# Attention quads in pairs on one Trainium2 core: scores alternate between row halves, weighing products between column halves

## What is computed

```python
def _L0_xattn_ref(q, k, v, Wq, bq, Wk, bk, Wv, bv, Wo, bo):
    Q = (q @ Wq.T + bq).reshape(bs, sl, H, HD)          # H = 16 heads of HD = 64
    K = (k @ Wk.T + bk).reshape(bs, sl, H, HD)
    V = (v @ Wv.T + bv).reshape(bs, sl, H, HD)
    score = jnp.einsum('bshd,bsgd->bshg', Q, K)         # 16 x 16 scores for each token
    weight = jax.nn.softmax(score, axis=-1)
    attn = jnp.einsum('bshg,bsgd->bshd', weight, V).reshape(bs, sl, nf)
    return attn @ Wo.T + bo

x = x + jnp.tanh(g_xattn[0]) * _L0_xattn_ref(_layernorm(x), ctx_2048, ctx_2048, ...)
x = x + jnp.tanh(g_ffn[0]) * _L0_ffn_ref(_layernorm(x), ...)   # shared part and 6 of 64 experts
```

## Time and profile before

| | us |
|---|---|
| median of 3 runs | 3447.93 |
| range of the runs | 3445.18 to 3456.05 |
| span of the profiled execution | 3457.1 |
| TensorE busy in it | 3292.0 (95%) |
| VectorE, ScalarE, GpSimd busy | 2301.2 (67%), 1615.1 (47%), 1339.3 (39%) |
| mean granted TensorE clock | 0.978 of full speed |

### The profile page before, as it was taken

How to read it: one execution, slowest core, us unless ns; L and a number is a source line. 1 busy time by engine, 2 the same in 40 slices (tenths; PEclk the granted TensorE clock), 3 DMA queues, 4 the chain that set the end, 5 groups by cost and what they waited for, 6 DMA issues and landing times. The chain is left out here.

```text
span 3457.1 us, 70136 instructions
## 1 busy us (share of the span) xinstructions
PE 3292.0 (95%) x24320; PEld 2195.9 (64%) x24320; DVE 2301.2 (67%) x3879; ACT 1615.1 (47%) x3324; POOL 1339.3 (39%) x1251
## 2 busy tenths in 40 slices
PE   6999999999999999779999998799999999999996
PEld 5888888888888888635555554455555555555553
DVE  7666666666666666657777775466666666666663
ACT  5555555555555555421111111355555555555552
POOL 1111111111111111134554454366666666566663
PEclk9999999999999999789999999899999999999998
DMA  5011111111111111053333331799999999999997
GB/s 195 26 38 38 38 39 38 39 38 39 38 39 38 39 38 44 32 195 111 108 97 99 114 104 56 230 298 305 295 307 298 309 295 311 271 295 309 297 306 156
DMA packets 206401, 515.20 MB, mean 149 GB/s; under 512 B 21216, under 2 KB 103136, under 8 KB 204128
## 3 DMA queue, kind: packets, MB, share of 16 engines
q0 software_dynamic: 79872, 268.68, 29.8%
q1 hardware_dynamic: 126304, 243.57, 20.1%
HBM read 322.97 MB, written 189.20 MB: 148 GB/s over the span
## 5 line engine op out<-in xcount | busy, mean ns | idle before, releaser
L635 PE MATMUL proj_ps<-ct_hi,wk_wv_hi 128*128 128x256 f16 x2048 | 561.0, 274 | 3.6 <-DVE wk_wv_lo L508 3.5
L636 PE MATMUL proj_ps<-ct_lo,wk_wv_hi 128*128 128x256 f16 x2048 | 559.3, 273 | 0.0
L637 PE MATMUL proj_ps<-ct_hi,wk_wv_lo 128*128 128x256 f16 x2048 | 559.2, 273 | 0.0
L1459 POOL DMA_INDIRECT out<-outs,target x256 | 402.3, 1572 | 302.3 <-ACT outs L1534 242.0
L1555 DVE TENSOR_TENSOR ext_lo<-eturn_ps,ext_hi 128x1024 f16<-128x1024 f32 x254 | 311.2, 1225 | 275.0 <-ACT ext_hi L1504 243.2
L332 POOL TENSOR_TENSOR probs<-probs,rsums 128x512 f32<-128x512 f32 x128 | 133.2, 1041 | 756.0 <-DVE rsums L534 756.0
L1430 POOL DMA_INDIRECT rows<-rows_dram,index x256 | 352.1, 1375 | 118.9 <-POOL index L1426 59.4
L1504 ACT ACTIVATE ext_hi<-eturn_ps 128x1024 f16<-128x1024 f32 x254 | 260.1, 1024 | 215.2 <-PE eturn_ps L1616 149.4
L407 ACT ACTIVATE probs<-probs,neg_max 128x128 f32<-128x128 f32 x512 | 199.1, 390 | 258.5 <-DVE neg_max L527 258.5
L635 PE MATMUL proj_ps<-xt_hi,wq_wo_hi 128*128 128x256 f16 x1024 | 283.2, 277 | 20.0 <-DVE whole L496 7.7
L1616 PE MATMUL eturn_ps<-ident,rows 128*128 128x128 f32 x2032 | 268.6, 276 | 34.6 <-DMA rows<-rows_dram,index 18.8
(11 more groups left out here) (185 smaller groups left out, 8240.2 us busy)
## 6 DMA issues: line engine op xcount, KB each, us to landing
ew_in<-w_up SPq DMA_DIRECT2D x64, 1024.0 KB
ew_in<-w_down SPq DMA_DIRECT2D x64, 512.0 KB
x_in<-x SPq DMA_DIRECT2D x16, 1024.0 KB, 7.0
c_in<-ctx_t SPq DMA_DIRECT2D x16, 1024.0 KB, 5.4
attn_dram<-attn SPq DMA_DIRECT2D x16, 1024.0 KB, 4.7
a_in<-attn_dram SPq DMA_DIRECT2D x32, 512.0 KB, 4.4
rx_in<-x SPq DMA_DIRECT2D x32, 512.0 KB, 4.1
rows_dram<-yn SPq DMA_DIRECT2D x32, 512.0 KB
```

Of the source, the lines that this page charges most:

```text
L635: pe.matmul(out, wh, hi[:, k, :], start=(k == 0), stop=False)
L636: pe.matmul(out, wh, lo[:, k, :], start=False, stop=False)
L637: last = pe.matmul(out, wl, hi[:, k, :], start=False, stop=(k == KC - 1))
L1459: pool.indirect_dma_start(out=out, out_offset=bass.IndirectOffsetOnAxis(ap=target[:, k:k + 1], axis=0), in_=outs[:, k, :], in_offset=None, ...
```

## The change

Scores and weighing products of two quads, 2i and 2i+1, are made together. The 24 score matmuls alternate between the quads, that is between the lower and the upper 64 rows of the array, and go to the two tiles `score_ps`. The 24 weighing matmuls alternate too; `attn_ps` now has 128 partitions, the even quad's result going to the lower 64 and the odd quad's to the upper 64, so that they use the two column halves of the array. The slots follow: the pairs' scores stand in slots 0, 6, 12, 18, values in the two slots after, turned 3 and 4 slots after, weighted for both 5 slots after; in the last step the pairs are 4 slots apart. The number of instructions is the same. Waits are now for both quads, and the counts of values before a turning of x follow the new slots.

```diff
--- before.py
+++ after.py
@@ -84,20 +84,26 @@
 CHUNKS = 3 * KC
 QKC = 2 * KC
 WHOLE = 4
-SLOT = [0, 2, 5, 8, 10, 13, 16, 18]
-ALONE = [0, 2, 4, 6, 8, 10, 12, 14]
+PAIR = [0, 6, 12, 18]
+PAIR_ALONE = [0, 4, 8, 12]
 TURN = [12, 20]
 WO_SPLIT = 10
 STATS = [3, 4]
 
 
+def values_at(q):
+
+    return PAIR[q // 2] + 1 + q % 2
+
+
 def work_after(n, proj):
 
     found = []
-    for q, s in enumerate(SLOT if proj else ALONE):
-        for stage, lag in (("weighted", 4 if proj else 5), ("turned", 3), ("values", 1), ("scores", 0)):
-            if s + lag == n:
-                found.append((stage, q))
+    for i, s in enumerate(PAIR if proj else PAIR_ALONE):
+        for odd in range(2):
+            for stage, lag in (("weighted", 5), ("turned", 3 + odd), ("values", 1 + odd), ("scores", 0)):
+                if s + lag == n:
+                    found.append((stage, 2 * i + odd))
     return sorted(found, key=lambda f: f[1])
 
 
@@ -152,7 +158,7 @@
         proj_ps = [ps(f"proj_ps{i}", [P, 512]) for i in range(2)]
         score_ps = [ps(f"score_ps{i}", [P, QUAD, P]) for i in range(2)]
         probs_ps = ps("probs_ps", [P, QUAD, P])
-        attn_ps = ps("attn_ps", [HD, QUAD, P])
+        attn_ps = ps("attn_ps", [P, QUAD, P])
 
         values_ps = turn_ps[:, 0:2, :].rearrange("p k (c d) -> p (k c) d", d=HD)
 
@@ -549,7 +555,7 @@
                     if q == 0:
 
                         dve.wait_ge(attn_stored[par], a.half().times(16))
-                    got = attn_ps[:].rearrange("d g (t o r) -> d r o (g t)", o=KC, r=2)
+                    got = attn_ps[half * HD:(half + 1) * HD].rearrange("d g (t o r) -> d r o (g t)", o=KC, r=2)
                     for r in range(2):
                         last = dve.tensor_copy(attn[r * HD:(r + 1) * HD, par, half, :, t0:t0 + TOK * QUAD],
                                                got[:, r])
@@ -607,7 +613,7 @@
                     pe.wait_ge(xt_lo_made, b.times(2, t))
 
                     if b.base >= 2:
-                        ahead = sum(s + 1 <= TURN[t] for s in SLOT)
+                        ahead = sum(values_at(q) <= TURN[t] for q in range(NQ))
                         pe.wait_ge(values_kept, b.plus(-2).times(NQ, ahead))
                     for k in range(KC):
                         last = pe.transpose(turn_ps[:, k, :], x_in[:, t, k * P:(k + 1) * P], ident[:])
@@ -647,26 +653,29 @@
                     return of[rows(q), t0:t0 + TOK, :].rearrange("d t h -> d (t h)")
 
                 def scores(a, q):
+
+                    if q % 2:
+                        return
                     if q == 0:
                         pe.wait_ge(qk_lo_made, a.times(QKC, QKC))
                         pe.wait_ge(even_kept, a.times(CHUNKS, CHUNKS))
                         pe.wait_ge(odd_kept, a.times(CHUNKS, CHUNKS))
 
-                    pe.wait_ge(masked_made, a.times(NQ, q - 1))
+                    pe.wait_ge(masked_made, a.times(NQ, q))
                     for g in range(QUAD):
-                        out = score_ps[q % 2][:, g, :]
-                        qh, ql = (group(part[:, a.base % 2, 0], q, g) for part in qk)
-                        kh, kl = (group(part[:, a.base % 2, 1], q, g) for part in qk)
-                        pe.matmul(out, qh, kh, start=True, stop=False)
-                        pe.matmul(out, qh, kl, start=False, stop=False)
-                        last = pe.matmul(out, ql, kh, start=False, stop=True)
-                    last.then_inc(scored, 1)
+                        for i, j in ((0, 0), (0, 1), (1, 0)):
+                            for half in range(2):
+                                made = pe.matmul(score_ps[half][:, g, :], group(qk[i][:, a.base % 2, 0], half + q, g),
+                                                 group(qk[j][:, a.base % 2, 1], half + q, g),
+                                                 start=(i == j), stop=(i == 1))
+                                if g == QUAD - 1 and i == 1:
+                                    made.then_inc(scored, 1)
 
                 def turn_values(a, q):
 
                     pe.wait_ge(values_kept, a.times(NQ, q))
 
-                    ahead = a.plus(2).times(2, sum(SLOT[q] + 1 > n for n in TURN))
+                    ahead = a.plus(2).times(2, sum(values_at(q) > n for n in TURN))
                     pe.wait_ge(xt_lo_made, min(ahead, 2 * NBLK) if isinstance(ahead, int) else ahead)
                     pe.sem_inc(apart, 1)
                     for g in range(QUAD):
@@ -682,17 +691,20 @@
                     last.then_inc(probs_turned, 1)
 
                 def weigh(a, q):
-                    pe.wait_ge(probs_kept, a.times(NQ, q + 1))
-                    pe.wait_ge(values_kept, a.times(NQ, q + 1))
+
+                    if q % 2:
+                        return
+                    pe.wait_ge(probs_kept, a.times(NQ, q + 2))
+                    pe.wait_ge(values_kept, a.times(NQ, q + 2))
 
                     pe.wait_ge(attn_kept, a.times(NQ, q))
                     for g in range(QUAD):
-                        vh, vl = (v[:, q % 2, g, :] for v in values)
-                        ph, pl = (p[:, q % 2, g, :] for p in probs_t)
-                        pe.matmul(attn_ps[:, g, :], vh, ph, start=True, stop=False)
-                        pe.matmul(attn_ps[:, g, :], vh, pl, start=False, stop=False)
-                        last = pe.matmul(attn_ps[:, g, :], vl, ph, start=False, stop=True)
-                    last.then_inc(attn_made, 1)
+                        for i, j in ((0, 0), (0, 1), (1, 0)):
+                            for half in range(2):
+                                made = pe.matmul(attn_ps[half * HD:(half + 1) * HD, g, :], values[i][:, half, g, :],
+                                                 probs_t[j][:, half, g, :], start=(i == j), stop=(i == 1))
+                                if g == QUAD - 1 and i == 1:
+                                    made.then_inc(attn_made, 1)
 
                 def first():
                     pe.wait_ge(ident_made, 2)
```

## The result

The change made the kernel slower: 3556.31 us median of four runs (3549.03 to 3564.22) against 3451.99 us of the kernel before on the same chip (3445.18 to 3467.03), a ratio of 1.0284 with a 95% interval of 1.0258 to 1.0309. The forecast was 3532 us, in a range of 3468 to 3588.

A forecast was written before the change was run, and what follows sets the result against it. TensorE was taken to bound the attention phase. A block gained 6.5 us, lost 9.7 to waits (net 2.7 taken) and 3.3 to the clock; 14 blocks gave 84 us, so 3532 us, range 3468 to 3588.

The forecast's parts named there:

- What bounds the kernel: Attention phase, 190 to 1430 us: TensorE sets the time, busy 1207.40 of 1240 us; nothing after that phase changes.
- The waits: New TensorE waits around the pairs and the turning of x, mostly on a shared PSUM tile: 9.7 us a block.
- The late VectorE: At the pair at slot 6, VectorE starts the masks 2.1 us late, making TensorE's wait 3.0 us.
- The gain on TensorE: Per block, 2.7 us from paired scores, 2.7 from paired weighing, 1.1 from fewer shape changes: 6.5 of 86.46 us.
- The weight loads: In paired weighing, 64 columns load in half the time of 128, 0.03 us, so pairing gains 2.7 us a block.
- rival B: Column halves, used in weighing, don't overlap, the rest as forecast: 40 us more, 3572 us; chance 0.20.
- The clock: After waits TensorE's clock halves for about 3.4 us, costing 1.7 us each time: 3.3 us a block.
- The sum: 14 blocks, each 2.7 us of waits less gain plus 3.3 of clock: 84 us more, 3532 us; chance 0.47.
- The last blocks: The fifteenth block and the last one, attention alone: each changes by 0, give or take 5 us.
- C: Waits are shorter or cost no clock: 3486 us, or 3456 with VectorE's lateness gone too; chance 0.16.
- D: Value transpositions and turning of x find their PSUM tile empty; with no waits 98 us less, 3350 us; chance 0.12.
- E: Pairs of scores and of weighing matmuls don't overlap at all: 80 us above forecast, 3612 us; chance 0.05.

The follow-up runs named there:

- e12: Changed kernel with the statistics of x moved to slots 8 and 9, normalization to 10 and 11: 3524.8 us, 1.021 of the kernel before.
- e1: Changed kernel with values of even and odd quads in separate banks of turn_ps: 3486.5 us, 1.008 of the kernel before.
- e3: Changed kernel with both separate value banks in turn_ps and x turned in slots 10 and 21: 3370.1 us, 0.974 of the kernel before.
- e6: e3 with the weighing matmuls quad after quad, scores still alternating: 3391.2 us, 0.981 of the kernel before.
- e7: e3 with the score matmuls quad after quad, weighing still alternating: 3394.3 us, 0.981 of the kernel before.
- e2: Changed kernel with x turned in slots 10 and 21 instead of 12 and 20: 3466.8 us, 1.004 of the kernel before.
- e5: Changed kernel with scores and weighing matmuls quad after quad, in the same slots: 3544.8 us, 1.026 of the kernel before.

## Why the prediction was right, and where it was off

**What bounds the kernel** held: the attention phase alone changed. By stretches, the 92.5 us are 14.0 before the first store, 88.6 for 13 periods, 2.9 for the rest of the phase (147.99 us against 145.15, up to 1584.10 and 1478.63), and -13 for the two later phases, which the change doesn't touch: over all profiled executions here they last between 1966 and 1981 us. The attention phase grew by 105 us; the forecast was 84.

**The waits**: right. In the block of 92.23 us the gaps, from 586.80 to 656.55 us, are longer than the normal 0.20 and 0.15 us by 0.89 (slot 2), 3.12 (slot 8), 3.80 (slot 13), 0.91 (slot 20) and 1.01 (turning): 9.7 us, where 0.9, 3.0, 3.8, 0.9 and 1.0 had been worked out. The late VectorE was 2.1 us as forecast, and e12 shows the statistics as its main part. The forecast said that it rested on the second quad's exponentials standing between scores and tile; the rows at slot 8 show them there. e1 to e3 confirm the tile.

**The gain on TensorE**: right as a sum. In the block of 92.23 us: 86.46 - 0.9 of old waits + 9.7 + 3.4 of clock (two stretches of 3.4 us at half speed) leaves 6.4 us, forecast 6.5. Its parts were ascribed wrongly, though. The forecast gave the overlap 5.4 us to alternation; e6 and e7 show 3.7 (8 bursts by 0.46), and the rest comes from two quads standing in one burst at all. It did not matter for the time, but it would for whoever keeps the pairs and drops the alternation.

**The weight loads.** Pairs of weighing products start every 0.056 us, so a load of 64 columns is done every 0.028 us on average, as the forecast's estimate wanted. The Trainium skill ("TensorE: Matmul & The Clock Gate", section "LDWEIGHTS (loading the stationary operand)") gives 53 ns for a load of 64 columns. The trace does not contradict that: within one column half the loads start 0.056 us apart, which leaves room for 53 ns each (from start to end one takes 110). What falls, and rival B with it, is the prediction's reading that by this rule a pair goes no faster than now: it put the loads of the two halves one behind the other, and they run side by side. The estimate came out right, but its reason, that half the columns load in half the time, is not what the rows show.

**The clock**: the mis-sized term. The forecast took 1.7 us for each fall and about two falls a block, 3.3 us. The number of falls was right: 29 in 13 periods, 2.2 a block, against 2 in all before. Twelve stand behind each of the waits at slots 8 and 13, four behind turns of the loop and one behind slot 20. But ten of them last 6.8 us instead of 3.4. Such a one, in the windows of the changed kernel:

```profile
1108.10:1114.70 6.60, 5.07 (x26) 3.69 (x27) 2.94 (x7) 1.65 (x5) 2.04 (x2) 0.50 0.01 2
```

The forecast had its 3.4 us from the earlier trace rows, behind a turn of the loop after which TensorE was busy for 2.95 of 3 us. In all ten long stretches the wait was not over when the clock fell: here, at slot 13, it went on for 1.5 us into the stretch, so that TensorE is busy for 5.07 of 6.60 us. In most of the nineteen short ones it had ended by then. That this is what prolongs the stretch was not tried by itself. So 10.2 us at half clock a block stand against 0.5, 4.9 us of matmuls, 1.6 more than counted.

The forecast weighed the waits at slots 8 and 13 with 0.75 and 1 fall a block; in the changed kernel both have 0.92. In e1, where the wait at slot 8 is gone, 12 of 13 blocks still have the fall at slot 13. In e2, where the one at slot 13 is gone, only 4 of 13 have one behind the same 3.1 us at slot 8, and five more falls follow turns of the loop. So the length of a wait alone does not tell whether the clock falls behind it; what else decides stays open.

**The sum.** Over 13 periods the growth is 6.8 us each, 4.9 of clock and 1.9 of waits less gain, where 3.3 and 2.7 had been counted: 10.6 us over the forecast. Ahead of the first store it is 14.0 where a block's 6.0 had been counted; from 80 us on the clock is 0.94 there, where it was 1.00, which is worth 7.2 of 120 us:

```profile
80.00:200.01 120.01, 109.61 (x1072) 93.27 (x1070) 71.09 (x153) 61.47 (x170) 13.85 (x13) 0.94 0.06 19
```

**The last blocks** were put at 0, give or take 5 each. Behind the fourteenth store the phase takes 2.9 us more, and 5.5 if one counts that this store now stands a slot (2.62 us) later. These three, 10.6, 8.0 and 2.9, make up the 21 us between 84 and 105.

**Rivals.** B is ruled out by the starts of attn_ps. C supposed that VectorE is in time or the clock holds; neither. D names the point from which it would decide, waits under 6.5 us a block; they are 9.7. e3 is D made true by hand, and gives 3370 where D said 3350: its gain is 6.4 less 1.4 of the wait for `whole`, its block 80.65. E was ruled out too, but its price was wrong as well: e5, with most of its overlap gone, is no slower, so the forecast's "80 us more" took an effect that was hidden behind waits for one on the path. The forecast added gains and waits as if they were independent of one another.

## What to carry to other kernels

Before two items of work are put side by side on one engine, follow the buffers that both fill on their way to the next engines: here a tile shared with a lag of one came free only after both items had gone through two in-order queues, and 9.7 us of waits ate a gain of 6.4 that was real. Such waits cost twice on TensorE, once as idle time and once by the clock behind them. Where the chain that ends the wait starts with the first item, making the pair faster gained nothing (e5); first free the tile, then pair (e3).

## What the runs showed of the hardware that was not expected

Matmuls of two row halves overlap by themselves at a change from one half to the other, by three or four matmuls, without being alternated in the program (e7: 1.09 us instead of 1.29 for 24), and those of two column halves do the same (e6: 1.12 us). Column halves of 64 overlap as fully as row halves, 24 in 0.64 us. More than half of a block's waits could be filled with unused matmuls at a profit: 48 of them of 256 columns a block, 5.6 us of TensorE's time, made the kernel 51 us faster. And while blocks follow one another (between the first and the fourteenth store), the clock stays at half for 3.4 us or 6.8; in the changed kernel for 6.8 only where the wait went on after the clock had fallen.
